# Start of a token-mixing and expert kernel: which queue asks for the first inputs, and where the weights' low half is made

## The chip, the cores and the metric

The kernel runs on one core of one Trainium2 chip. The metric is the device time of one execution in microseconds (us). Before the change the median of three runs is 468.17 us (466.95 to 468.71). The engines are TensorE (PE in the profile; PEld is its weight load), VectorE (DVE), ScalarE (ACT), GpSimd (POOL) and SyncE (SP). Each has an instruction queue of its own, and they meet only at semaphores.

## The reference

The input x has the shape (8, 192, 16, 16): eight batches of 256 tokens with 192 channels. A first layer normalises each token, mixes tokens with a chunked delta rule (12 heads of 16, chunks of 16 tokens) and adds the result. A second layer normalises again and adds a mixture of 8 experts, two per token. Only the start of the first layer matters here:

```
x = x + conv(_ln_c(x))                # _ln_c: (v - mean) / sqrt(var + 1e-6) over the channels

t = x.reshape(B, C, L).transpose(0, 2, 1)
q = l2norm(heads(silu(t @ Wq)))
k = l2norm(heads(silu(t @ Wk)))
v = heads(silu(t @ Wv))
beta = sigmoid(t @ Wb)
o = delta_rule_chunked(q, k, v, beta) # then @ Wo, added to t
```

## The kernel before, in words

Tokens lie in 16 tiles of 128 (`x_sb`, 128 partitions by 16 tiles by 192 channels); a step of the first layer handles the two tiles of one "batch" b, for b = 0 to 7. `PARTS` (line 200) cuts x in two: tiles 0 to 3, which serve b = 0 and 1, and tiles 4 to 15.

Precision comes from splitting float32 values into two float16 halves. The projection weights `wqkvb_sb` (96 partitions, 2 halves of the channels, 588 columns: 384 for k and v, 204 for q and beta) are scaled by `WSCALE` = 64. `wqh` is the float16 rounding of that, `wql` the rest. Tokens are split the same way into `tTh` and `tTl`. Each projection is a sum of three products (`tTh`·`wqh`, `tTl`·`wqh`, `tTh`·`wql`) for each half of the channels, so 24 products for a batch: 12 for each of its two tiles.

Nothing plans the order: each engine runs the list written for it, in that order.

- **SyncE** (lines 296 to 304) first calls `start_at_one` (208 to 213), which adds one to every semaphore of the stage, and only then asks for the first part of x, the projection weights (302), the constants (303), the second part of x and `wo` (304). All waits count from ONE, so a wait for a transfer is a wait for ONE + 16.
- **GpSimd** sets small constants (`eps_c`, lines 353 and 354) and later adds x to the tokens (370) and squares keys and queries (378, 380).
- **ScalarE** (411 to 426) waits for `eps_c`, runs a one-element Sqrt so that the sqrt table is loaded early, waits for the weights, writes `wqh` (423), scales the weights in place (424), takes the square root of the first variances in `deviation(0)` (417), and runs a one-element Silu (426), so that the next table is loaded. After that it turns transposed tokens into `tTh` (433) and reads the products out (443 to 451).
- **VectorE** (488 to 515 and 599 to 606) takes the statistics of the first part of x in `moments(0)` (502, 228 to 233), waits for the scaled weights, writes `wql` (515), takes the reciprocal of the deviation (510), waits for the constants, writes the normalised tokens `tw` of batches 0 and 1 (525), then `tTl` of both (536), and then takes the statistics of the second part.
- **TensorE** (614 to 684) waits for the constants, which hold the identity matrix, transposes the tokens of batches 0 and 1 (624), waits for `wql`, and multiplies (633).

After the first projections comes a loop over b, in which scores are formed and stored; a second stage runs the recurrence over chunks, and the last stage, from about 297 us on, runs the experts (lines 1495 to 1655).

Of the kernel before, what the change touches and what calls it, by code (L numbers as in the profile page):

```python
# [20 lines left out]
NT = B * L // TP  # L21
# [28 lines left out]
ONE = 1  # L50
WSCALE = 64.0
# [4 lines left out]
def program(nc, x, consts, wqkvb, wo, gate, wfc, bias, wproj, out):  # L56
    f32, f16 = mybir.dt.float32, mybir.dt.float16
    ALU, ACT, AX = mybir.AluOpType, mybir.ActivationFunctionType, mybir.AxisListType
    ds = bass.ds
    ctx = ExitStack()  # L60
    with ctx:
        def sb(name, shape, dt=f32):
            return ctx.enter_context(nc.sbuf_tensor(name, shape, dt))

        semaphores = []
# [3 lines left out]
        def sem(name):  # L69
            semaphores.append(held_by[0].enter_context(nc.semaphore(name)))  # L70
            return semaphores[-1]

        s_cst = sem("s_cst")
# [17 lines left out]
        cst = sb("cst", [128, CW])  # L91
        ident = cst[:, ID0:ID0 + 128]
        x_sb = sb("x_sb", [128, NT, C])
# [106 lines left out]
        PARTS = ((0, 4), (4, NT))  # L200
        s_x, s_w, s_wo = sem2("s_x"), sem("s_w"), sem("s_wo")
# [4 lines left out]
        started = [0]  # L206

        def start_at_one(eng, end=None):

            end = len(semaphores) if end is None else end  # L210
            for s in semaphores[started[0]:end]:
                eng.sem_inc(s, ONE)
            started[0] = end

# [20 lines left out]
        with ExitStack() as mix:  # L235
# [7 lines left out]
            wqkvb_sb = sbm("wqkvb_sb", [HC, 2, KVW + QBW])  # L243
            wqh = sbm("wqh", [HC, 2, KVW + QBW], f16)
            wql = sbm("wql", [HC, 2, KVW + QBW], f16)
# [14 lines left out]
            tT_high, wq_high, wq_low = sem("tT_high"), sem("wq_high"), sem("wq_low")  # L260
# [29 lines left out]
            s_inv = sem("s_inv")  # L290
            ln_ld = sem("ln_ld")

            with nc.Block() as block:

                @block.sync
                def _(sp):
                    start_at_one(sp)
                    for part, (lo, hi) in enumerate(PARTS):
                        sp.dma_start(x_sb[:, lo:hi, :], x.rearrange("p (t c) -> p t c", t=NT)[:, lo:hi, :])\
                            .then_inc(s_x[part], 16)  # L300
                        if part == 0:
                            sp.dma_start(wqkvb_sb[:, :, :], wqkvb.rearrange("p (a n) -> p a n", a=2)).then_inc(s_w, 16)
                            sp.dma_start(cst[:, :], consts).then_inc(s_cst, 16)
                    sp.dma_start(wo_sb[:, :, :], wo.rearrange("p (a n) -> p a n", a=2)).then_inc(s_wo, 16)

                    def store_kvq(b, u, n):

                        by_constant(sp, b + 1, n + 1)
                        sp.wait_ge(kn_done, ONE + b + 1)
                        sp.dma_start(d_kv[ds(2 * b, 2), :, :].rearrange("t p c -> p t c"),  # L310
                                     kvw[u][:, :, :, :].rearrange("p t h d -> p t (h d)")).then_inc(st_kv[u], 16)
                        sp.dma_start(d_q[ds(2 * b, 2), :, :].rearrange("t p c -> p t c"),
                                     qw[u][:, :, :, :].rearrange("p t h d -> p t (h d)")).then_inc(st_q[u], 16)

                    def step(b, u, n, ahead):
                        for j in range(2):
                            if j and ahead:
                                store_kvq(b + 1, 1 - u, n + u)

                            by_constant(sp, b + 1)  # L320
                            sp.wait_ge(n_ready[j], ONE + b + 1)
                            sp.dma_start(d_n[ds(2 * b + j, 1), :, :].rearrange("t p c -> (t p) c"),
                                         nw[j][:, :, :, :].rearrange("p a r i -> p (a r i)")).then_inc(st_n[j] if b + 1 < B else end_n, 16)
                            sp.dma_start(d_pt[ds(2 * b + j, 1), :, :].rearrange("t p c -> (t p) c"),
                                         ptw[j][:, :, :, :].rearrange("p a r i -> p (a r i)")).then_inc(st_pt[j] if b + 1 < B else end_p, 16)

                    store_kvq(0, 0, 0)
                    for b in range(B):
                        if b + 1 == B:
                            sp.wait_ge(s_inv, ONE + 2 * (CH - 1))  # L330
                            for c in range(DEEP):
                                load_inverse(sp, c)
                        step(b, b % 2, b // 2, 2 if b + 2 < B else 1 if b + 1 < B else 0)
                        if b == 3:
                            for j in range(2):
                                sp.wait_ge(st_n[j], ONE + 16 * (b + 1))
                            load_lanes(sp, lane_n, 0, ln_ld)
                        if b == 5:
                            for c in range(DEEP):
                                load_kv(sp, c)  # L340
                                load_q(sp, c)
                                load_p(sp, c)
                    sp.wait_ge(s_wo, ONE + 16)
                    for u in range(2):
                        sp.wait_ge(st_kv[u], ONE + 16 * (B // 2))
                        sp.wait_ge(st_pt[u], ONE + 16 * (B - 1))
                        sp.wait_ge(st_n[u], ONE + 16 * (B - 1))
                        sp.wait_ge(st_q[u], ONE + 16 * (B // 2))
# [60 lines left out]

                @block.scalar  # L410
                def _(act):
                    act.wait_ge(s_eps, ONE + 2)

                    def deviation(part):
# [5 lines left out]

                    nc.scalar.activation(early_s[:, 0:1], eps_c[0:1, 0:1], ACT.Sqrt)
                    act.wait_ge(s_w, ONE + 16)
                    nc.scalar.activation(wqh[:, :, :], wqkvb_sb[:, :, :], ACT.Copy, scale=WSCALE)
                    nc.scalar.activation(wqkvb_sb[:, :, :], wqkvb_sb[:, :, :], ACT.Copy, scale=WSCALE).then_inc(wq_high, 1)
                    deviation(0)
                    nc.scalar.activation(early_s[:, 1:2], eps_c[0:1, 0:1], ACT.Silu)

# [61 lines left out]
                def _(dve):  # L489
# [17 lines left out]
                    def inverse_deviation(part):  # L507
                        lo, hi = PARTS[part]
                        dve.wait_ge(s_sq, ONE + part + 1)
                        nc.vector.reciprocal(rstd[:, lo:hi], rstd[:, lo:hi]).then_inc(s_rs, 1)  # L510
                        dve.wait_ge(s_rs, ONE + part + 1)

                    moments(0)
                    dve.wait_ge(wq_high, ONE + 1)
                    nc.vector.tensor_tensor(wql[:, :, :], wqkvb_sb[:, :, :], wqh[:, :, :], ALU.subtract).then_inc(wq_low, 1)
                    inverse_deviation(0)
                    dve.wait_ge(s_cst, ONE + 16)

                    def tokens(b, u):

                        if not first_use(b):
                            dve.wait_ge(tT_filled, ONE + b - 1)
                            dve.wait_ge(t_added, ONE + b - 1)
                        for j in range(2):
                            last = nc.vector.tensor_scalar(tw[u][:, j, :],
                                                           x_sb[:, ds(2 * b + j, 1), :].rearrange("p t c -> p (t c)"),
                                                           mean[:, ds(2 * b + j, 1)], rstd[:, ds(2 * b + j, 1)],
                                                           ALU.subtract, ALU.mult)
                        last.then_inc(t_ready, 1)

                    def low_t(b, u):

                        dve.wait_ge(tT_high, ONE + b + 1)
                        if not first_use(b):
                            dve.wait_ge(qb_done, ONE + 2 * b - 2)
                        nc.vector.tensor_tensor(tTl[u][:, :, :, :].rearrange("p a b n -> p (a b n)"),  # L536
                                                ps[0:HC, tT_bank(b), :],
                                                tTh[u][:, :, :, :].rearrange("p a b n -> p (a b n)"), ALU.subtract)\
                            .then_inc(tT_out, 1)
# [58 lines left out]

                    tokens(0, 0)
                    tokens(1, 1)  # L600
                    low_t(0, 0)
                    low_t(1, 1)
                    moments(1)
# [1 line left out]
                    dve.wait_ge(pads, ONE + 2)  # L605
                    norm(0, 0)
                    inverse_deviation(1)
                    for b in range(B):
                        step(b, b % 2, b // 2, 2 if b + 2 < B else 1 if b + 1 < B else 0)

# [605 lines left out]
        key = sbr("key", [128, NT, E])  # L1216
# [512 lines left out]
```

## Time and profile before

| | |
|---|---|
| runs | 468.17 us median; 466.95 to 468.71 |
| the profiled execution | 469.37 us |
| its span, from the first to the last instruction | 467.6 us |
| mean granted TensorE clock | 0.83 of full speed |
| busy share PE, DVE, ACT, POOL | 77%, 61%, 40%, 54% |
| DMA | 48.85 MB, 104 GB/s on average |

The profile is of one execution. Times in its timeline are us from the first instruction. "Busy" leaves out the instructions that only issue transfers or count semaphores; in the timeline transfers that are issued by SyncE and ScalarE stand as SPq and ACTq, with the time that the issue took. An arrow `[7.28 <-DMA x_sb<-x]` says how long the engine was idle before the instruction and what ended that. A mark `out<-in` names the tensors written and read, `x4` how many like instructions were merged in the row.

### The profile page before, as it was taken

How to read it: one execution, taken by the hardware profiler on the slowest of the kernel's cores; microseconds unless marked ns; L12 is line 12 of the kernel's file. 1: busy time of each engine (PE TensorE's matmuls, PEld its weight loads, DVE VectorE, ACT ScalarE, POOL GpSimd, SP SyncE). 2: the span in 40 equal slices, each digit the busy share in tenths (PEclk: the TensorE clock that was granted, in tenths of full speed). 3: DMA queues.
4: the chain of work that ended last, by engine and by line, in shares of the span. 5: the costliest groups of instructions: out<-in, count | busy, mean ns of one | idle time of the engine just before them, and what ended most of it. 6: DMA issues, size and time to landing. Idle time of an engine off the chain costs nothing. (4 is left out here: it accounts for less than half of the span.)

```text
span 467.6 us, 20003 instructions
## 1 busy us (share of the span) xinstructions
PE 360.2 (77%) x8080; PEld 291.0 (62%) x8080; DVE 283.3 (61%) x627; ACT 187.4 (40%) x433; POOL 253.9 (54%) x309
## 2 busy tenths in 40 slices
PE   0878988665469799999973711799999999999980
PEld 0555665443357587777752511689989989987760
DVE  2776688686224467777766679356575576563440
ACT  3386666541324547777753610122313322311110
POOL 1262224995699954555544501727877786674221
PEclk9977797776555769999995555599999999999986
DMA  5013237153877266788641330213433333333111
GB/s 206 13 60 109 100 125 220 42 166 109 191 188 201 69 187 179 234 239 240 193 148 38 102 138 0 77 18 63 58 54 62 53 61 52 48 44 48 19 12 14
DMA packets 38929, 48.85 MB, mean 104 GB/s; under 512 B 12790, under 2 KB 34886, under 8 KB 38616
## 3 DMA queue, kind: packets, MB, share of 16 engines
q0 software_dynamic: 10288, 20.06, 20.3%
q1 hardware_dynamic: 27994, 26.26, 18.3%
q10 hardware_dynamic: 592, 1.77, 1.4%
q8 instruction: 38, 0.62, 0.6%
q14 instruction: 17, 0.14, 0.1%
HBM read 30.05 MB, written 16.45 MB: 99 GB/s over the span
## 5 line engine op out<-in xcount | busy, mean ns | idle before, releaser
L1655 POOL DMA_INDIRECT out<-yo,give x39 | 68.0, 1744 | 49.1 <-DVE yo L1627 38.8
L1510 PE MATMUL ps<-xs,w_up 128*128 128x256 f16 (+1 forms) x552 | 78.0, 259 | 2.7 <-issue 2.6
L1510 PEld LDWEIGHTS ps<-xs,w_up 128*128 x552 | 53.1, 98 | 13.5 <-issue 4.3
L1567 ACT ACTIVATE xb<-xs 64x256 f16<-64x256 f16 (+1 forms) x23 | 8.8, 384 | 130.5 <-DVE xs L1590 130.5
L1634 POOL DMA_INDIRECT row<-d_x,take x39 | 39.4, 1009 | 35.3 <-DVE take L1381 23.7
L1627 DVE TENSOR_SCALAR yo<-ps,slot_gate 128x192 f32<-128x192 f32 x39 | 14.8, 414 | 51.2 <-PE ps L1530 51.2
L1619 DVE TENSOR_TENSOR hl<-hw,hh 128x512 f16<-128x512 f32 (+1 forms) x69 | 42.6, 618 | 2.4
L1530 PE MATMUL ps<-pjh,hh 128*128 x234 | 42.9, 250 | 0.4 <-DVE hl L1619 0.4
L1530 PE MATMUL ps<-pjh,hl 128*128 x234 | 42.6, 249 | 0.0
L1530 PE MATMUL ps<-pjl,hh 128*128 x234 | 42.5, 249 | 0.0
L806 POOL TENSOR_SCALAR kx<-kvt,cst 128x192 f32<-128x192 f32 x32 | 29.5, 934 | 17.0 <-PE ps L1107 16.8
L1510 PE MATMUL ps<-xb,w_up 66*128 66x256 f16 (+1 forms) x138 | 35.8, 259 | 0.0
L1579 ACT ACTIVATE hw<-ps 128x512 f32<-128x512 f32 (+1 forms) x69 | 31.3, 514 | 6.6 <-PE ps L1510 6.6
L1617 DVE CAST hh<-hw 128x512 f16<-128x512 f32 (+1 forms) x69 | 29.1, 422 | 2.8 <-ACT hw L1579 2.8
L670 PE MATMUL ps<-kqT 16*32 16x64 f32 x1536 | 21.1, 241 | 11.1 <-DVE gm L572 8.8
L378 POOL TENSOR_TENSOR sqw<-kvw 128x384 f32<-128x384 f32 x8 | 6.6, 826 | 40.2 <-ACT beta L451 32.8
L670 PEld LDWEIGHTS ps<-kqT 16*32 16x32 f32 x1536 | 17.2, 109 | 15.7 <-issue 15.1
L633 PE MATMUL ps<-wqh,tTh 96*128 96x384 f16 (+1 forms) x64 | 24.3, 380 | 2.1 <-DVE tTl L536 1.5
L633 PE MATMUL ps<-wqh,tTl 96*128 96x384 f16 (+1 forms) x64 | 24.4, 381 | 0.0
L633 PE MATMUL ps<-wql,tTh 96*128 96x384 f16 (+1 forms) x64 | 24.1, 376 | 0.0
L1530 PEld LDWEIGHTS ps<-pjh,hh 128*128 128x128 f16 x234 | 20.6, 99 | 4.5 <-issue 3.7
L1128 PE MATMUL ps<-uo,pt 32*32 32x16 f32 x1536 | 17.9, 186 | 5.7 <-issue 5.7
(238 smaller groups left out, 896.5 us busy)
## 6 DMA issues: line engine op xcount, KB each, us to landing
pjs<-wproj POOLq DMA_DIRECT2D x7, 576.0 KB, 7.5
d_kv<-kvw SPq DMA_DIRECT2D x8, 384.0 KB, 2.5
d_pt<-w_up SPq DMA_DIRECT2D x16, 192.0 KB, 2.4
kvt<-d_kv SPq DMA_DIRECT2D x16, 192.0 KB, 3.6
pt<-d_pt SPq DMA_DIRECT2D x16, 192.0 KB, 3.6
x_sb<-wfc POOLq DMA_DIRECT2D x8, 384.0 KB, 5.8
fcs<-wfc POOLq DMA_DIRECT2D x6, 384.0 KB, 4.9
d_q<-qw SPq DMA_DIRECT2D x8, 192.0 KB, 2.7
```

Of the source, the lines that this page charges most:

```text
L633: last = nc.tensor.matmul(ps[:, bank, 0:width], ts[u][:, j, hf, :], ws[:, hf, first:first + width], start=(k == 0), stop=(k == 5))
L670: last = nc.tensor.matmul(ps[cols, 4 + q, 64 * a:64 * a + 64], kqT[j][rows, a, 0, cols], kqT[j][rows, a, :, cols], start=True, stop=True)
L806: last = nc.gpsimd.tensor_scalar(dst[:, :, a, :].rearrange("p g (h d) -> p g h d", d=D), src.rearrange("p (g h) d -> p g h d", g=HG), cst[ ...
L1128: last = nc.tensor.matmul(ps[rows, 5, C + D * h:C + D * h + D], pt[u][rows, h, :], uo[u][rows, D * h:D * h + D], start=False, stop=False, ...
L1510: last = nc.tensor.matmul(ps[:, NP * u + m // 2, (m % 2) * n:(m % 2 + 1) * n], w[k][:, m * 128:(m + 1) * 128], x, start=(k == 0), stop=(k ...
L1530: last = nc.tensor.matmul(y[half], hs[u][:, m // 2, at:at + TP], ws[:, m * C:(m + 1) * C], start=False, stop=(m == HB - 1 and k == 2), ski ...
L1579: nc.scalar.activation(hw[u][:, i, 0:2 * width(s)], ps[:, NP * u + i, 0:2 * width(s)], ACT.Gelu_apprx_tanh, scale=1.0 / WSCALE).then_inc(h ...
L1617: nc.vector.tensor_copy(hh[u][:, i, 0:n], hw[u][:, i, 0:n]).then_inc(hh_done, 1)
L1619: nc.vector.tensor_tensor(hl[u][:, i, 0:n], hw[u][:, i, 0:n], hh[u][:, i, 0:n], ALU.subtract)\
L1627: nc.vector.tensor_scalar(yo[s % YB][:, half, :], ps[:, 6, half * C:(half + 1) * C], slot_gate[:, at:at + 1], None, ALU.mult).then_inc(yo_ ...
L1634: nc.gpsimd.indirect_dma_start(row[s % RB][:, half, :], None, d_x.rearrange("p t c -> (p t) c"), bass.IndirectOffsetOnAxis(ap=take[:, at:a ...
L1655: nc.gpsimd.indirect_dma_start(out, bass.IndirectOffsetOnAxis(ap=give[:, at:at + 1], axis=0), yo[s % YB][:, half, :], None, compute_op=ALU ...
```

## The change

The three loads that are needed first (the first part of x, the projection weights, the constants) are issued by ScalarE, ahead of its first wait. SyncE keeps the second part of x and `wo`. `start_at_one` raises the same semaphores, now with those of the three loads last. ScalarE no longer scales the weights in place; VectorE computes `wql` as weights times `WSCALE` minus `wqh` in one scalar_tensor_tensor, after the tokens of batches 0 and 1 and ahead of their `tTl`. VectorE's wait for the constants moves from ahead of the tokens to just ahead of the loop over b.

```diff
         def start_at_one(eng, end=None):
             end = len(semaphores) if end is None else end
-            for s in semaphores[started[0]:end]:
+            inputs = [s_cst, s_w, s_x[0]]
+            for s in sorted(semaphores[started[0]:end], key=lambda s: inputs.index(s) if s in inputs else -1):
                 eng.sem_inc(s, ONE)
             started[0] = end
...
+            def load_x(eng, part):
+                lo, hi = PARTS[part]
+                eng.dma_start(x_sb[:, lo:hi, :], x.rearrange("p (t c) -> p t c", t=NT)[:, lo:hi, :])\
+                    .then_inc(s_x[part], 16)
...
                 def _(sp):
                     start_at_one(sp)
-                    for part, (lo, hi) in enumerate(PARTS):
-                        sp.dma_start(x_sb[:, lo:hi, :], x.rearrange("p (t c) -> p t c", t=NT)[:, lo:hi, :])\
-                            .then_inc(s_x[part], 16)
-                        if part == 0:
-                            sp.dma_start(wqkvb_sb[:, :, :], wqkvb.rearrange("p (a n) -> p a n", a=2)).then_inc(s_w, 16)
-                            sp.dma_start(cst[:, :], consts).then_inc(s_cst, 16)
+                    load_x(sp, 1)
                     sp.dma_start(wo_sb[:, :, :], wo.rearrange("p (a n) -> p a n", a=2)).then_inc(s_wo, 16)
...
                 def _(act):
+                    load_x(act, 0)
+                    act.dma_start(wqkvb_sb[:, :, :], wqkvb.rearrange("p (a n) -> p a n", a=2)).then_inc(s_w, 16)
+                    act.dma_start(cst[:, :], consts).then_inc(s_cst, 16)
                     act.wait_ge(s_eps, ONE + 2)
...
                     act.wait_ge(s_w, ONE + 16)
-                    nc.scalar.activation(wqh[:, :, :], wqkvb_sb[:, :, :], ACT.Copy, scale=WSCALE)
-                    nc.scalar.activation(wqkvb_sb[:, :, :], wqkvb_sb[:, :, :], ACT.Copy, scale=WSCALE).then_inc(wq_high, 1)
+                    nc.scalar.activation(wqh[:, :, :], wqkvb_sb[:, :, :], ACT.Copy, scale=WSCALE).then_inc(wq_high, 1)
...
                     moments(0)
-                    dve.wait_ge(wq_high, ONE + 1)
-                    nc.vector.tensor_tensor(wql[:, :, :], wqkvb_sb[:, :, :], wqh[:, :, :], ALU.subtract).then_inc(wq_low, 1)
                     inverse_deviation(0)
-                    dve.wait_ge(s_cst, ONE + 16)
...
                     tokens(0, 0)
                     tokens(1, 1)
+                    dve.wait_ge(wq_high, ONE + 1)
+                    nc.vector.scalar_tensor_tensor(wql[:, :, :], wqkvb_sb[:, :, :], WSCALE, wqh[:, :, :],
+                                                   ALU.mult, ALU.subtract).then_inc(wq_low, 1)
                     low_t(0, 0)
                     low_t(1, 1)
...
                     inverse_deviation(1)
+                    dve.wait_ge(s_cst, ONE + 16)
                     for b in range(B):
```

## Rows read from the trace of the kernel before

**Rows 1.** The page's part 4, the chain that ended last, by line.
```profile
PE ps L1510 17%; PE ps L1530 13%; PE ps L1495 2%; PE ps L1522 1%; DVE x_sb L1354 1%; DMA d_x<-x 1%; DMA out<-yo,give 1%; POOL row L1634 1%; SPq L1249 1%; DMA row<-d_x,take 1%; DVE of_tile L1360 0%; POOL out L1655 0%; DVE of_tile L1357 0%; DVE xl L1271 0%; PE ps L1431 0%
```

**Rows 2.** Waits of 0 to 30 us: us in total, times, longest.
```profile
PE ps L624 <- DVE tw L525: 13.4, 1, 13.4
...
DVE st_sb L502 <- DMA x_sb<-x: 7.3, 1, 7.3
```

**Rows 3.** Timeline of 0 to 25 us: start, us, engine, line, instruction.
```profile
0.77 1.28 ACT L421 ACT_TABLE_LOAD   x1 [0.77 <-PEq L1721]
...
3.70 0.41 SPq L299 DMA_DIRECT2D x_sb<-x  x1
4.17 0.41 SPq L302 DMA_DIRECT2D wqkvb_sb<-wqkvb  x1
...
7.28 1.14 DVE L502 BATCH_NORM_STATS2 st_sb<-x_sb 128x6 f32<-128x192 f32 x4 [7.28 <-DMA x_sb<-x]
...
8.82 1.18 ACT L423 ACTIVATE wqh<-wqkvb_sb 96x1176 f16<-96x1176 f32 x1 [6.56 <-DMA wqkvb_sb<-wqkvb]
...
9.45 0.16 DVE L233 SCALAR_TENSOR_TENSOR tmpa<-tmpb,tmpa 128x4 f32<-128x4 f32 x1
9.91 1.17 ACT L424 ACTIVATE wqkvb_sb<-wqkvb_sb 96x1176 f32<-96x1176 f32 x1
10.98 0.28 ACT L417 ACTIVATE rstd<-tmpa,eps_c 128x4 f32<-128x4 f32 x1
11.11 1.38 DVE L515 TENSOR_TENSOR wql<-wqkvb_sb,wqh 96x1176 f16<-96x1176 f32 x1 [1.50 <-ACT wqkvb_sb L424]
...
12.41 0.17 DVE L510 RECIPROCAL rstd<-rstd 128x4 f32<-128x4 f32 x1
...
12.61 1.93 DVE L525 TENSOR_SCALAR tw<-x_sb,mean,rstd 128x192 f32<-128x192 f32 x4
...
13.43 2.26 PE L624 MATMUL ps<-cst,tw 128*96 128x128 f32 x8 [13.43 <-DVE tw L525]
...
14.53 0.59 ACT L433 ACTIVATE tTh<-ps 96x512 f16<-96x512 f32 x1 [1.75 <-PE ps L624]
...
15.15 0.69 DVE L536 TENSOR_TENSOR tTl<-ps,tTh 96x512 f16<-96x512 f32 x1 [0.61 <-ACT tTh L433]
...
15.94 0.48 PE L633 MATMUL ps<-wqh,tTh 96*128 96x384 f16 x1 [0.26 <-issue]
...
16.96 3.20 DVE L502 BATCH_NORM_STATS2 st_sb<-x_sb 128x6 f32<-128x192 f32 x12
...
18.84 0.52 PE L633 MATMUL ps<-wqh,tTh 96*128 96x384 f16 x1
```

**Rows 4.** Line 763 alone, loads of 576 KB: issue durations, and us to landing.
```profile
L763 ACTq DMA_DIRECT2D pjs<-wproj x1: 453/453/453, 140.4 to 140.4; - x1
...
DMA to landing us min/median/max: 6.3/7.5/10.8
```

**Rows 5.** DMA issues of 0 to 30 us: KB each, median us to landing.
```profile
x_sb<-x SPq DMA_DIRECT2D x1, 1152.0 KB, 7.5
...
cst<-consts SPq DMA_DIRECT2D x1, 377.0 KB, 5.1
```

**Rows 6.** Busy time by stretch: PE, PEld, DVE, ACT, POOL, granted clock, DMA share, GB/s.
```profile
4.00:4.50 0.50, 0.00 (x0) 0.00 (x0) 0.00 (x0) 0.00 (x0) 0.00 (x0) 1.00 0.00 0
```

**Rows 7.** VectorE's instructions grouped by line and shape: busy us, mean ns.
```profile
L881 DVE SCALAR_TENSOR_TENSOR pjl<-pjs,pjh 128x1152 f16<-128x1152 f32 x8 | 10.7, 1343 | 0.0
```

**Rows 8.** Timeline again, 23 to 25 us.
```profile
23.92 1.28 ACT L459 ACT_TABLE_LOAD   x1
...
24.17 0.95 DVE L543 TENSOR_REDUCE ssw<-sqw 128x48 f32<-128x768 f32 x1 [2.76 <-POOL sqw L380]
```

**Rows 9.** Busy time by stretch, columns as in rows 6.
```profile
19.00:21.00 2.00, 2.00 (x9) 0.96 (x7) 1.85 (x9) 0.41 (x3) 0.00 (x0) 1.00 0.00 0
21.00:23.00 2.00, 2.00 (x15) 1.51 (x14) 0.35 (x2) 0.92 (x4) 0.47 (x1) 1.00 0.00 0
```

## The prediction

> **What bounds the kernel now.** I began with the chain that ended last [rows 1]: it names TensorE's expert products, which are not touched. A start-up saving can still reach the end, provided the first products start sooner and nothing after them has a clock of its own. So I read the waits of the first 30 us [rows 2]: TensorE's longest is 13.4 us, for VectorE's normalised tokens `tw`, and VectorE's is 7.3 us, for the first part of x. Then the timeline, in order [rows 3]. The reader is to see one chain there: SyncE's first ask at 3.70, x at VectorE at 7.28, statistics done at 9.45 + 0.16 = 9.61; ScalarE's square root of them only at 10.98, because it stands behind two weight copies (8.82 and 9.91) that waited 6.56 us for the weights; VectorE's reciprocal only at 12.41, because it stands behind `wql` (11.11, 1.38 us); `tw` at 12.61, the first transpose at 13.43, `tTl` at 15.15, the first projection product at 15.94. The reciprocal is the only consumer of that square root and could have begun near 11.26.
>
> **The asks.** SyncE asks only at 3.70, though the other engines work from 0.77 [rows 3]; what lies ahead on its queue are 50 semaphore increments (I count the names), some 0.06 us each. ScalarE's queue is free at 0.77, and the three asks there stand ahead of its first wait. I put x there at 0.77 in place of 3.70, 2.93 us sooner. ScalarE's own asks later in this kernel took 0.453 us [rows 4], about SyncE's spacing (4.17 - 3.70 = 0.47), so I put the weights at 1.23, 2.94 sooner than 4.17, and the constants at 1.69. With the delays of before (3.58 and 4.65 to first use, 5.1 to the constants' landing [rows 5]) VectorE starts at 4.35, ScalarE's copy at 5.88, and the constants are there at 6.8. The semaphore increments for these three now come last on SyncE, near 3.7, still 0.65 us before x lands. The delays have bounds, as no row shows a load from ScalarE's queue this early: nothing moves up to 4.5 us [rows 6], so below, they could stay as they are (no gain from the asks, worked out as a rival); above, a large load from ScalarE or GpSimd landed in 6.3 to 10.8 us late in the kernel [rows 4]. I take the early rows themselves: same tensors, same idle engines.
>
> The second part of x stays on SyncE, now first there, at 3.70. With its old 7.5 us [rows 5], which included the queue of three transfers ahead of it, it lands at 11.2. Its reader, the second statistics (16.96 before), comes at 12.0 in my sum: hidden, with 0.8 to spare. `wo` is asked for sooner too, and no row of these 30 us reads it.
>
> **The small parts.** The sqrt table load (1.28 us at 0.77 [rows 3]) and its first ACTIVATE move behind the three asks, to about 2.15; they end by 3.65, and the weights arrive at 5.88, so it costs nothing unless the load is placed ahead of the asks (a rival). The second copy (1.17 us) goes. The first runs 5.88 to 7.06, its successor can follow after 9.91 - 8.82 = 1.09, at 6.97. Statistics end at 9.61 - 2.93 = 6.68, so the square root starts at 6.97 and ends at 7.25 (0.28). The reciprocal follows at 7.28, `tw` 0.20 later at 7.48: 5.13 us sooner. Here the saving is largest: 2.93 of asks, 2.20 of waiting behind copy and `wql`. VectorE no longer waits for the constants before `tw`; TensorE's own wait for them stays ahead of its transposes, at 7.48 + 0.82 = 8.30, and 6.8 covers it.
>
> **What is given back.** `wql` is now one scalar_tensor_tensor between tokens and `tTl`. VectorE's wait for `wqh` (done 7.06) costs nothing. Its price: the nearest rows are 1.38 us for the two-input form on the same shape [rows 3] and 1343 ns for this form on 1152 columns [rows 7], scaled by 1176/1152 to 1.37; I take 1.38, and the bounds are these two. Before, tokens took 12.61 to 14.54, so they now end at 9.41, `wql` ends at 10.79, and `tTl` can begin at 10.72 (the reciprocal began 0.08 before `wql`'s end). `tTh` is ready 14.53 + 0.59 - 13.43 = 1.69 after the first transpose, at 9.99, so `wql` is what ends last there and gives back 0.73. The Silu table load (7.25 to 8.53) is hidden behind the transposes. Queued behind `wql` are both `tTl` and the second statistics, and TensorE waits for the first `tTl`. First product: 10.72 + 0.79 = 11.51 against 15.94, **4.43 us sooner**. The second statistics follow at about 12.0, 4.9 sooner, so they are not late.
>
> **The sum.** The profiled run took 469.37 us (span 467.6 and 1.77 around it), 1.2 above the median of 468.17. From it, 469.37 - 4.43 = 464.9; from the median, **463.8**, which I give. Everything after the first product hangs on products, on VectorE or on transfers that those release, so I expect the shift to be kept.
>
> **Rivals.** (1) The sqrt table is loaded ahead of the asks. For: the load at 23.92 runs before the sums its ACTIVATE waits for (24.17 to 25.12) are there [rows 8], so loads do run ahead of waits. Against: there no ask stood between. Asks begin at 2.05, all of the above 1.28 later: gain 3.15, 465.0.
>
> (2) TensorE's clock rises later relative to its work. The rows of 19 to 21 and 21 to 23 us print a granted clock of 1.00 both times, yet 9 matmuls and then 15 fill them [rows 9]: the pace changes in between, from the 1.2 to the 2.4 GHz level, after TensorE has been at the transposes since 13.43 and at products since 15.94. If the rise came at the same instant as before in spite of the earlier products, the second pair's first half would run slow. It was 12 products, of 2.9 us at the low pace (18.84 - 15.94) [rows 3, 9] and about 1.5 at the high one; ScalarE's lengths, which stand behind its output, would be 1.35 late: gain 3.1, 465.1. The Trainium skill (TensorE: Matmul & The Clock Gate, Part 1) says that the point of the rise moves from run to run; one trace here can't show it. An earlier rise would add to the gain by up to about 1.5.
>
> (3) The change doesn't do what it says: ScalarE's queue is not served before the time at which it was served for SyncE. For: nothing moves until 4.5 [rows 6]. Against: SyncE's spacing explains that by itself. Only the reordering is left: x at 7.28, weights copied 8.82 to 10.00, square root 9.91, reciprocal 10.22, `tw` 10.42, `wql` from 12.35, `tTl` 13.66 against 15.15: gain 1.5, 466.7. The Trainium skill speaks for this (DMA: Bandwidth & Descriptors, Issuing engines are not separate DMA queues): a second issuing engine only saves the sequencer's issue time. By that rule x, which had no ask ahead of it, would not come sooner, and the time would be this rival's; the increments ahead of the ask in this trace are why I don't follow it.
>
> (4) Slower: the weights come late on ScalarE's queue, now that x's second part is served from another queue beside them. Since the square root stands behind the weight copy and VectorE's `wql` ahead of `tTl`, each us of it is a us of the gain. It decides at a weights' landing past 5.88 + 4.43 = 10.3. At the longest row, 10.8 us [rows 4], they land at 12.0: square root 13.1, `tw` 13.6, `tTl` 16.85 against 15.15, 1.7 lost, 469.9. Against: x's second part is asked for 2.5 us after them.
>
> **How the numbers follow.** About 0.5%, 2.3 us, is what a measurement of this kernel can tell from no change. Forecast 0.62; (1) 0.13; (2) 0.10: all three faster by more, 0.85. (3) 0.11: within. (4) 0.04: slower. The range reaches down to 463.8 - 1.5 for an early rise and 0.4 for the spread of the runs, 461.9, and up to (2) and (1) with 0.9 for the spread, 466.0; (3) and (4), 0.15, are left out.
>
> **What would show it.** ScalarE's first ask near 0.8 and the table load behind the third (else (1)); first statistics near 4.4 (7.3 would be (3)); copy near 5.9 (past 10, (4)); `tw` near 7.5; `wql` 1.4 us and directly ahead of `tTl`, `tTl` without a wait for `tTh`; first product near 11.5, and each later landmark earlier by the same. The forecast is wrong if the first product comes sooner by 4 us and the end does not.

## The result and the profile after

The changed kernel takes 466.68 us in the median of 20 runs (461.39 to 471.61), the kernel before 470.32 us in the median of 20 runs of the same sessions (466.95 to 474.17). The ratio is **0.991, with a 95% interval of 0.9885 to 0.9935**; it leaves out runs more than 1.5% above the fastest of their kernel, three of the changed kernel's among them, so it is not quite that of the two medians (0.9923). The change makes the kernel faster by about 0.9%; 463.8 of 468.17, as forecast, is a ratio of 0.9907. The forecast time, 463.8 us with a range of 461.9 to 466.0, was too low all the same: the measured 466.68 lies 0.7 us above the range. So there are two questions: was the mechanism the one that was forecast, and what was wrong with the number?

The timeline of the changed kernel's profiled execution (466.81 us, span 464.9) from 0 to 25 us, with the columns of [rows 3]:

```profile
0.76 0.40 ACTq L296 DMA_DIRECT2D x_sb<-x  x1
...
1.19 0.45 ACTq L414 DMA_DIRECT2D wqkvb_sb<-wqkvb  x1
1.67 0.45 ACTq L415 DMA_DIRECT2D cst<-consts  x1
2.15 1.28 ACT L425 ACT_TABLE_LOAD   x1 [2.15 <-issue]
...
3.71 0.41 SPq L296 DMA_DIRECT2D x_sb<-x  x1
...
4.43 1.14 DVE L505 BATCH_NORM_STATS2 st_sb<-x_sb 128x6 f32<-128x192 f32 x4 [4.43 <-SPq L213]
...
5.93 1.18 ACT L427 ACTIVATE wqh<-wqkvb_sb 96x1176 f16<-96x1176 f32 x1 [2.29 <-DMA wqkvb_sb<-wqkvb]
...
7.02 0.28 ACT L421 ACTIVATE rstd<-tmpa,eps_c 128x4 f32<-128x4 f32 x1
...
7.33 0.18 DVE L513 RECIPROCAL rstd<-rstd 128x4 f32<-128x4 f32 x1 [0.57 <-ACT rstd L421]
7.55 1.93 DVE L524 TENSOR_SCALAR tw<-x_sb,mean,rstd 128x192 f32<-128x192 f32 x4
...
8.36 2.26 PE L627 MATMUL ps<-cst,tw 128*96 128x128 f32 x8 [8.36 <-DVE tw L524]
...
9.40 1.37 DVE L601 SCALAR_TENSOR_TENSOR wql<-wqkvb_sb,wqh 96x1176 f16<-96x1176 f32 x1
9.46 0.59 ACT L436 ACTIVATE tTh<-ps 96x512 f16<-96x512 f32 x1 [0.64 <-PE ps L627]
...
9.56 2.06 POOL L371 TENSOR_TENSOR r_sb<-x_sb,tw 128x384 f32<-128x384 f32 x1 [0.20 <-DVE tw L524]
...
10.70 1.28 DVE L535 TENSOR_TENSOR tTl<-ps,tTh 96x512 f16<-96x512 f32 x2
...
11.47 0.48 PE L636 MATMUL ps<-wqh,tTh 96*128 96x384 f16 x1 [0.85 <-DVE wql L601]
...
11.89 3.20 DVE L505 BATCH_NORM_STATS2 st_sb<-x_sb 128x6 f32<-128x192 f32 x12
...
14.61 0.33 ACT L452 ACTIVATE qw<-ps 128x192 f32<-128x192 f32 x1 [0.53 <-PE ps L636]
...
15.32 0.42 PE L636 MATMUL ps<-wqh,tTh 96*128 96x384 f16 x1
...
15.59 0.33 PE L636 MATMUL ps<-wqh,tTl 96*128 96x384 f16 x1
...
17.17 0.82 POOL L379 TENSOR_TENSOR sqw<-kvw 128x384 f32<-128x384 f32 x1 [5.55 <-ACT kvw L446]
```

Read it against [rows 3]. ScalarE asks at 0.76, 1.19 and 1.67, and its table load stands behind the asks, at 2.15. The idle time before the copy has fallen from 6.56 to 2.29 us. The square root follows the one copy at once, the reciprocal follows the square root at once, and `wql` is directly ahead of `tTl`, which no longer waits for `tTh`. The row of the first statistics names SyncE's increments (line 213) as what it waited for; that mark is inferred, and since SyncE is through with them before its ask at 3.71, what was still missing was x, which by the next rows landed 3.6 us after its ask. The first product comes at 11.47 in place of 15.94, 4.47 us sooner.

The issues of 0 to 30 us in the changed kernel, with KB and us to landing as in [rows 5]:

```profile
x_sb<-x SPq DMA_DIRECT2D x1, 1152.0 KB, 6.0
wqkvb_sb<-wqkvb ACTq DMA_DIRECT2D x1, 441.0 KB, 4.7
x_sb<-x ACTq DMA_DIRECT2D x1, 384.0 KB, 3.6
...
cst<-consts ACTq DMA_DIRECT2D x1, 377.0 KB, 5.1
```

ScalarE's loads take what SyncE's took (3.6, 4.6 and 5.1 us in the trace before). The second part of x lands at 3.71 + 6.0 = 9.7, over 2 us ahead of its reader.

And yet the two profiled executions end only 467.6 - 464.9 = 2.7 us apart. The start gained 4.47, so 1.8 us seem to be lost on the way. This is what the experiments were about.

### The profile page after: what moved, and what is told of

Its sections match the earlier page's. It is cut to its first block and busy times, and to the rows that moved or that the text cites. A ratio compares the mean times of both kernels' runs of the same rounds, so it can differ in the third digit from the quotient of the medians.

```text
span 464.9 us, 20002 instructions
## 1 busy us (share of the span) xinstructions
PE 360.1 (77%) x8080; PEld 290.1 (62%) x8080; DVE 286.5 (62%) x627; ACT 186.5 (40%) x432; POOL 255.8 (55%) x309
## 3 DMA queue, kind: packets, MB, share of 16 engines
q1 hardware_dynamic: 27594, 25.03, 17.7%
## 5 line engine op out<-in xcount | busy, mean ns | idle before, releaser
L809 POOL TENSOR_SCALAR kx<-kvt,cst 128x192 f32<-128x192 f32 x32 | 30.5, 964 | 16.8 <-PE ps L1110 16.6
L1070 PE MATMUL ps<-kvt,mb 32*32 32x32 f32 x1536 | 19.6, 208 | 2.9 <-issue 2.9
```

The costliest lines, as they stand in the source:

```text
L809: last = nc.gpsimd.tensor_scalar(dst[:, :, a, :].rearrange("p g (h d) -> p g h d", d=D), src.rearrange("p (g h) d -> p g h d", g=HG), cst[ ...
L1070: last = nc.tensor.matmul(ps[rows, 4, 32 * h:32 * h + 32], mb[u][rows, h, :, :].rearrange("p c i -> p (c i)"), kvt[u][rows, h, :], start=T ...
```

## The experiments

**Theory A**: the start's gain is carried whole, and the end of one execution wanders with TensorE's clock. **Theory B**: some 45% of it is lost in the loop. Every kernel was timed in five rounds beside the kernel before, on the same chip.

**The changed kernel again** (`again`, `again_2`, `again_3`; no edit).

> The changed kernel once more, nothing edited. Theory A (the start's gain is carried whole; the end of one execution wanders with TensorE's clock in the first layer's loop): first projection product at 11.5 us as before, the lead over the kernel before differs along the loop and at the end from the first profile's (it was 4.47 us at the first product and 2.5 us in the expert stage), and over the rounds the ratio is near 0.9905 (4.47 of 470). Theory B (a fixed part of the gain is lost in the loop, as the one pair of profiles seems to show): the lead again falls to about 2.5 us in the expert stage, and the ratio is near 0.9945.

> The changed kernel a third time. Theory A: ratio near 0.9905 again (0.991 and 0.9899 so far), first product at 11.5 to 11.8 us, the lead in the expert stage anywhere within 3 us of 4.4. Theory B: 0.9945.

> The changed kernel a fourth time, beside the next two on the same chip: ratio 0.9905, first product at 11.5 to 11.8 us.

Ratios: 0.9899 (0.9859 to 0.994), 0.9904 (0.9871 to 0.9936) and 0.9891 (0.9862 to 0.9921). First products at 11.74, 11.53 and 11.71. With the first comparison, weighted by runs (20, 6, 6 and 6), the ratio is 0.9904, near A's 0.9905. B's 0.9945 lies outside each of the four intervals. But a single execution ends anywhere: the spans are 464.9, 467.1, 468.5 and 465.8 us for one and the same kernel. So it is the timed runs that speak for A. The profiles by themselves would not: on average the four of the changed kernel lie 4.4 us ahead of the two of the kernel before (the second is under `before_again`) at the first product, but 1.6 us ahead at the first products of the expert stage (298.5 against 300.1) and 2.3 us at the end.

**The kernel before again** (`before_again`; no edit).

> The kernel before, nothing edited, timed against itself. First product at 15.9 us again. Theory A (what wanders is TensorE's clock from execution to execution, so single times spread by several us and a median of three runs can be off by 2 us): ratio 1.000 within 0.004, single runs 467 to 474 us, and a profile whose loop runs ahead of or behind the first one's by 1 us or more though its start is the same. Rival (the first three runs, 466.95 to 468.71, were the kernel's true level): a median near 468.

Ratio 1.0053 (1.0021 to 1.0085), median 473.19 of 10 runs. The rival is out: nothing is near 468; the kernel before had medians of 472.12, 471.42 and 472.13 in the three later sessions. A's 1.000 within 0.004 is missed too: the same program differs from itself by 0.5%, with an interval that leaves out 1. That is about what a comparison of six to twelve runs is good for here, and no ratio below can be read more finely. First product at 16.08.

How far single executions part is read best from one landmark late in the chain that ended last (start, us, what): the first products of the expert stage. For the first profile of the kernel before:

```profile
299.05 8.12 PE ps L1510 x60
```

for `before_again`:

```profile
301.14 8.63 PE ps L1510 x60
```

for the changed kernel's first profile:

```profile
296.55 8.12 PE ps L1513 x60
```

and for `again_2`:

```profile
300.91 8.57 PE ps L1513 x60
```

So `again_2` reaches the experts 4.4 us after its twin, though it began 0.06 later at the first product, and `before_again` 2.1 us after its twin, though it began 0.14 later. Busy time by stretch, with the columns of [rows 6], says what differs late in the run; the sixth figure after the length is the granted clock. First for the changed kernel's first profile:

```profile
190.00:235.00 45.00, 41.41 (x1986) 33.45 (x1983) 34.50 (x63) 33.74 (x81) 24.91 (x41) 1.00 0.75 222
235.00:300.00 65.00, 27.68 (x417) 21.78 (x418) 45.06 (x138) 19.77 (x49) 21.69 (x38) 0.55 0.21 71
300.00:310.00 10.00, 10.00 (x101) 8.59 (x99) 5.25 (x11) 3.05 (x6) 1.25 (x2) 1.00 0.08 22
```

then for `again_2`:

```profile
190.00:235.00 45.00, 41.70 (x1951) 34.33 (x1952) 33.39 (x59) 31.72 (x77) 23.80 (x38) 0.94 0.75 216
235.00:300.00 65.00, 28.25 (x426) 21.97 (x425) 45.16 (x139) 20.74 (x50) 19.43 (x37) 0.50 0.21 71
300.00:310.00 10.00, 9.59 (x72) 7.48 (x70) 4.00 (x8) 2.21 (x5) 3.99 (x5) 0.77 0.19 51
```

One program, and the granted clock averages 0.55 in one execution and 0.50, the 1.2 GHz level throughout, in the other from 235 to 300 us, and 1.00 or 0.77 under the first expert products. The changed kernel's first profile had the better clock in each of these three stretches. That the clock makes the whole of the difference is not shown: over the 38 timed runs of the changed kernel the time and the mean granted clock go together only loosely (a correlation of -0.5). Either way, 2.7 us between two single profiles is no measure of what was carried.

**The two parts, each alone** (`asks_only`, `asks_only_2`; `order_only`, `order_only_2`). As edits of the changed kernel: the loads from ScalarE, with the old copies and low half:

```diff
-                    nc.scalar.activation(wqh[:, :, :], wqkvb_sb[:, :, :], ACT.Copy, scale=WSCALE).then_inc(wq_high, 1)
+                    nc.scalar.activation(wqh[:, :, :], wqkvb_sb[:, :, :], ACT.Copy, scale=WSCALE)
+                    nc.scalar.activation(wqkvb_sb[:, :, :], wqkvb_sb[:, :, :], ACT.Copy, scale=WSCALE).then_inc(wq_high, 1)
...
                     moments(0)
+                    dve.wait_ge(wq_high, ONE + 1)
+                    nc.vector.tensor_tensor(wql[:, :, :], wqkvb_sb[:, :, :], wqh[:, :, :], ALU.subtract).then_inc(wq_low, 1)
                     inverse_deviation(0)
+                    dve.wait_ge(s_cst, ONE + 16)
...
-                    dve.wait_ge(wq_high, ONE + 1)
-                    nc.vector.scalar_tensor_tensor(wql[:, :, :], wqkvb_sb[:, :, :], WSCALE, wqh[:, :, :],
-                                                   ALU.mult, ALU.subtract).then_inc(wq_low, 1)
...
-                    dve.wait_ge(s_cst, ONE + 16)
                     for b in range(B):
```

and the loads back on SyncE, with the new copies and low half:

```diff
-            inputs = [s_cst, s_w, s_x[0]]
-            for s in sorted(semaphores[started[0]:end], key=lambda s: inputs.index(s) if s in inputs else -1):
+            for s in semaphores[started[0]:end]:
...
                     start_at_one(sp)
+                    load_x(sp, 0)
+                    sp.dma_start(wqkvb_sb[:, :, :], wqkvb.rearrange("p (a n) -> p a n", a=2)).then_inc(s_w, 16)
+                    sp.dma_start(cst[:, :], consts).then_inc(s_cst, 16)
                     load_x(sp, 1)
...
                 def _(act):
-                    load_x(act, 0)
-                    act.dma_start(wqkvb_sb[:, :, :], wqkvb.rearrange("p (a n) -> p a n", a=2)).then_inc(s_w, 16)
-                    act.dma_start(cst[:, :], consts).then_inc(s_cst, 16)
```

> The kernel before with the three loads asked for by ScalarE, and the old order of copies and low half. By the steps: copies at 5.93 and 7.02, square root 8.09, low half 8.22 to 9.60, reciprocal 9.52, tokens 9.72, tTl 12.26, first product 13.05, 2.9 us sooner than before. Theory A: ratio 0.994 (2.9 of 470). Theory B (some 55% carried): 0.9965.

> The three loads from ScalarE alone, a second time: it came out at 0.9896 though its first tokens are only 2.6 us sooner. Theory A: that was the spread of six runs, and together with this one the ratio moves to 0.994, with first transposes at 10.8 us again. Rival: the asks alone bring all of the gain, and the ratio stays at 0.990.

> The changed kernel with the three loads asked for by SyncE again, in the old order; copies and low half as changed. By the steps: x at 7.28, copy 8.82, square root 9.91, reciprocal 10.22, tokens 10.42, low half from 12.35, tTl 13.66, first product 14.45, 1.5 us sooner than before. Theory A: ratio 0.997. Theory B: 0.998. The two parts should then add to the whole: 2.9 and 1.5 are 4.4.

> The new order of copies and low half alone, a second time (0.9969 so far). Theory A: 0.997, first product 1.5 us sooner than before. Rival (the order alone brings nothing, the asks all): 1.000.

The asks alone: ratios 0.9896 (0.9858 to 0.9934) and 0.9959 (0.9933 to 0.9986); by their 6 and 12 runs, 0.9938. First products at 13.32 and 12.85 (13.05 forecast). The order alone: 0.9969 (0.9939 to 1.0) and 0.9976 (0.9954 to 0.9998), together 0.997; first products at 14.28 and 14.94 (14.45 forecast). The first 0.9896 would by itself have made the asks the whole of the gain; its repeat shows what six runs are worth. The parts add up: 0.6% and 0.3% make the 0.9 to 1.0% of the whole. Of the times that is a fit and no proof, since 0.3% is less than the kernel before differed from itself; at the first product, where the traces part them, the asks bring 2.6 and 3.1 us and the order 1.7 and 1.0, for 4.2 to 4.5 of both.

**An earlier first product** (`early_products`): `wql` moved behind the first `tTl`, and TensorE's first 12 products reordered, so that `tTh` and `wqh` need not wait for `wql`.

```diff
+                    low_t(0, 0)
                     dve.wait_ge(wq_high, ONE + 1)
...
-                    low_t(0, 0)
                     low_t(1, 1)
...
+                    def first_products():
+                        for ready, ts, ws in ((tT_high, tTh, wqh), (tT_out, tTl, wqh), (wq_low, tTh, wql)):
+                            pe.wait_ge(ready, ONE + 1)
...
-                    pe.wait_ge(wq_low, ONE + 1)
-                    project(0, 0)
+                    first_products()
+                    project(0, 0, (1,))
```

> The changed kernel with the low half of the weights after the first tTl, and TensorE's first 12 products in another order: the four of tTh and wqh as soon as tTh is there, then tTl and wqh, then tTh and wql last. First product near 10.2 (1.3 us sooner than the changed kernel's 11.47), first half of the low-half products at 12.1, the first tile's queries read out at about 13.4 in place of 14.61, second statistics later by 0.7 us and not missed. Theory A: 1.2 us sooner than the changed kernel at the end, ratio to the kernel before 0.988. Rival: wql ends last for the first tile and nothing is won, ratio as of the changed kernel.

Ratio 0.989 (0.9853 to 0.9926): no better than the changed kernel. Its timeline from 0 to 26 us:

```profile
13.41 0.49 ACT L446 ACTIVATE kvw<-ps 128x384 f32<-128x384 f32 x1 [2.01 <-PE ps L648]
13.80 0.32 ACT L452 ACTIVATE qw<-ps 128x192 f32<-128x192 f32 x1
...
16.16 0.49 ACT L446 ACTIVATE kvw<-ps 128x384 f32<-128x384 f32 x1 [1.97 <-PE ps L636]
...
17.71 0.83 POOL L379 TENSOR_TENSOR sqw<-kvw 128x384 f32<-128x384 f32 x1 [7.01 <-issue]
```

The products began at 10.57, 0.90 sooner than in the changed kernel's first profile (in which x landed 0.24 sooner), and the first tile's queries were read out at 13.80 in place of 14.61. But the second tile's products wait for the first one's readout, and the squares come at 17.71, against 17.17 there and 17.75 in `again`. The rival holds, by another mechanism than it named: what ends last is the second tile at the low pace, not `wql`.

**TensorE at work ahead of the first projections** (`warm`, `warm_early`). The extra products change no result.

```diff
                 def _(pe):
+                    zeros = qn[0][:, :, :, :].rearrange("p a h d -> p (a h d)").bitcast(f16)
+                    pe.wait_ge(pads, ONE + 2)
+                    for k in range(10):
+                        nc.tensor.matmul(ps[:, 4, :], zeros[:, 0:TP], zeros[:, 0:512], start=True, stop=True)
                     pe.wait_ge(s_cst, ONE + 16)
```

> The changed kernel with ten extra TensorE products (128x512, on a block of zeros that GpSimd sets at the start, into an unused bank) ahead of the wait for the constants; they change no result. They start near 3.7 us and are done before the first transpose at 8.4. In the two kernels so far the pace of the products doubled 8.3 us (before: 13.43 to 21.8) and 7.1 us (changed: 8.36 to 15.5) after TensorE's first work. Theory C (TensorE's low clock at the start is what the first projections now pay for, and any work ahead of them brings the rise forward): pace doubles near 11 to 12 us, the first squares on GpSimd come 1.5 us sooner than 17.2 to 17.8, ratio 0.987. Rival (work on zeros, or the gap before the transposes, leaves the clock where it was): pace doubles near 15.5 to 16.5 and the ratio stays 0.9905.

> The same ten products ahead of the kernel with the low half after the first tTl and the reordered first 12 products, whose ratio was 0.989. Theory C: the first products start at 10.2 and run at the high pace soon after, squares near 15, ratio 0.985. Rival: no better than the reordered kernel, 0.989.

Ratios 0.994 (0.9917 to 0.9963) and 0.9938 (0.9905 to 0.9971), beside 0.9891 for the changed kernel on the same chip: **no better**, against the theory. They are 0.5% above the changed kernel, as much as the kernel before differed from itself, so that the extra products make it slower is not shown. In `warm`, the timeline from 0 to 26 us:

```profile
3.40 4.45 PE L619 MATMUL ps<-qn 128*128 128x512 f16 x10 [3.40 <-SPq L213]
...
8.69 0.61 PE L631 MATMUL ps<-cst,tw 128*96 128x128 f32 x4 [0.84 <-DVE tw L524]
```

and busy time by stretch (columns as above):

```profile
8.00:11.00 3.00, 1.26 (x8) 0.78 (x8) 3.00 (x5) 2.18 (x4) 2.10 (x2) 1.00 0.47 178
11.00:14.00 3.00, 2.20 (x8) 1.19 (x9) 3.00 (x10) 0.22 (x2) 0.95 (x1) 0.58 0.00 0
14.00:17.00 3.00, 3.00 (x15) 1.86 (x13) 2.46 (x12) 0.95 (x4) 0.00 (x0) 0.50 0.00 0
17.00:20.00 3.00, 2.94 (x19) 1.94 (x18) 0.00 (x0) 1.56 (x6) 1.59 (x3) 0.78 0.00 0
```

The clock does rise before the transposes: the first four of them take 0.61 us, against 2.26 for the eight in the changed kernel. (The 1.00 in 8 to 11 us would not tell by itself, as the column shows it at the low pace of [rows 9] too.) It falls again to the 1.2 GHz level just as the products begin (0.58 and 0.50 from 11 to 17), after a stretch in which TensorE had only eight transposes, and comes back in 17 to 20. So the rise under the products was not brought forward, nor left where the rival put it: their pace doubles near 18.2 us, against 15.4 in the changed kernel's first profile and 17.7 in `again_2`, and the first tile's products run at the low pace in all of them. A loss at the end does not show in this profile: its first expert products start at 298.49, those of the changed kernel's four profiles at 298.5 on average.

In `warm_early`'s profile the clock stays up over the first products, whose groups of four start 0.50 us apart (0.98 in `early_products`), and the next engine is late instead; its timeline from 0 to 26 us:

```profile
10.05 0.67 PE L652 MATMUL ps<-wqh,tTh 96*128 96x384 f16 x4
...
10.55 0.66 PE L652 MATMUL ps<-wqh,tTl 96*128 96x384 f16 x4
...
15.28 0.82 POOL L379 TENSOR_TENSOR sqw<-kvw 128x384 f32<-128x384 f32 x1 [4.70 <-ACT kvw L446]
...
16.07 0.83 POOL L381 TENSOR_TENSOR sqw<-qw 128x384 f32<-128x384 f32 x1
...
16.18 2.06 DVE L230 TENSOR_SCALAR mean<-mean 128x12 f32<-128x12 f32 x1
...
16.83 1.38 POOL L363 MEMSET pjl<- 128x1536 f32 x1
...
18.99 0.94 DVE L542 TENSOR_REDUCE ssw<-sqw 128x48 f32<-128x768 f32 x1
```

The squares come 1.9 us sooner than in the changed kernel (15.28 against 17.17) and are done by 16.90, but VectorE, still busy with the second statistics, sums them only at 18.99, 0.2 later than there (18.81). What holds it up is one small operation of these statistics: on 128 by 12 elements it took 2.06 us, to 18.24, where it took 0.17 in the changed kernel. It ran beside GpSimd's squares and the fill behind them (to 18.21); why it was so long no run isolates. Nor is that the end of it: at the first product of the third batch this profile leads the changed kernel's first one again by 1.4 us (29.27 against 30.66), and at the first expert products, at 298.92, it lies among the four (296.55 to 300.91). None of the three extensions is better than the changed kernel.

## Why the prediction was right and wrong

**The asks.** Right: first ask at 0.76 (0.77), statistics at 4.43 (4.35), copy at 5.93 (5.88). The rows of SyncE's loads were the right price for ScalarE's, and the increments ahead of SyncE's first ask were what the loads had waited for: in `warm` TensorE's first wait, for a semaphore that is the 45th of the 50, ended at 3.40 with SyncE's increment of it, and SyncE's first ask came at 3.71, so the five left took 0.06 us each, as forecast. (No run left the asks on SyncE and put them ahead of the increments.) Alone, this part brings its first product to 13.32 and 12.85 and 0.6% in the time.

**The small parts and what is given back.** Right, in the first profile each within 0.11 us: square root 7.02 (6.97), tokens 7.55 (7.48), `wql` 1.37 (1.38) and 9.40 to 10.77, `tTl` 10.70 (10.72), first product 11.47 (11.51). The statistics of the second part start at 11.89 (12.0) and wait for nothing. One term off the chain was too long: the second part of x landed at 9.7, not at 11.2, which nothing felt. Alone, the order brings 1.0 to 1.7 us at the first product and 0.3%.

**Is the shift kept?** On the average of the runs, yes. First products of four profiles of the changed kernel come at 11.61 on average, of two of the kernel before at 16.01: 4.4 us, 0.93% of 471.5, the mean of the four medians of the kernel before. The four ratios, weighted by runs, average 0.9904. A and B lie only 0.4% apart, less than the kernel before differed from itself, so it is that four comparisons agree (0.9891 to 0.991) that decides. The lost 1.8 us of the first pair of profiles is less than the repeats without an edit part by. That it was clock is not shown: the clock was not held fixed in any run.

**The step that failed is the last sentence of the sum**: "from the median, **463.8**, which I give". The median of three runs, 468.17, was taken as the kernel's level, and "0.4 for the spread of the runs" and "0.9 for the spread" as its uncertainty. With all 20 runs that level is 470.32, and in three more sessions it is 471.4 to 472.1. Less 4.43, 470.32 gives 465.9 for a measured 466.68. The mechanism was right; the mis-sized term is the base, by 2.2 of the 2.9 us that the forecast was off (in the other 0.7 these two medians lie 3.64 apart and not 4.43), and with it the allowance: the 20 single runs of the kernel before lie between 466.95 and 474.17, the first three lay low among them (bad luck, as far as the record shows), and their own spread, 466.95 to 468.71, gave no sign of it. The profiled run's own base, 469.37, would have given 464.9, inside the stated range but still low.

**The rivals.** (1) is out: the table load stands at 2.15, behind the asks. (2) is open from one execution to the next: in the first profile the rise came 7.0 us after the first transpose (15.4 less 8.36) in place of 8.3, so not later relative to the work; in `again_2` it came 9.3 us after it (17.7 less 8.42), and GpSimd's squares at 18.14 in place of 17.17, 1.0 us late where (2) had priced 1.35. That the rise moves from run to run is borne out: with first products at 11.5 to 11.7 in all four, TensorE put 18, 17, 14 and 17 matmuls into the stretch of 14 to 17 us. The Trainium skill (TensorE: Matmul & The Clock Gate, Part 1) says the same of kernel starts, and these profiles agree. (3) is out: x came at 4.43, and what was saved was SyncE's other work ahead of the ask. The rule of the Trainium skill (DMA: Bandwidth & Descriptors, Issuing engines are not separate DMA queues), that a second issuing engine saves only the time of the issue, did not describe this start. (4) is out: the weights landed at 5.9.

## What to carry to other kernels

A first load waits for everything that its queue does ahead of it: look for a queue that is free at the start, and for work that stands between a transfer's landing and the operation on the critical chain. Price such a move from the same tensors' rows in the trace of before; here every landmark of the chain came out within 0.11 us in the first profile, and the first product within 0.23 in its repeats. But state the result as a difference or a ratio, and take the base and its spread from many runs: the difference of two single profiles (2.7 us here, for a shift of 4.4) and a median of three runs (2.2 us off here) are both less certain than a change of this size.

## What the runs showed that was not expected

Ten extra TensorE products ahead of the first projection did not make the kernel faster (0.994, beside 0.9891 for the changed kernel): in the profile the clock rose early, fell again around the short transposes, and was low under the first tile's products, as it is without the extra work.

GpSimd's second addition of 128 by 384 float32 elements took 2.06 us in the changed kernel's profile, where it began at 9.56 beside `wql` (9.40 to 10.77), and 2.06 in `order_only`, where it also stood beside it. Where `wql` came earlier (`asks_only`) or later (`early_products`) it took 0.99. No engine waited for it.
